# Retention on one Trainium2 core: gate projection split in halves, group deviation by a power on GpSimd

## The reference, cut to what matters

```
qkv = x @ w_qkv; q, k, v = split(qkv)          # x is the layer norm of the residual stream
q = xpos(q); k = xpos(k)                       # rotary tables, 16 heads of 32 columns
scores = einsum('bhtd,bhsd->bhts', q, k) * D ** (-0.5) * decay_mask
y = einsum('bhts,bhsd->bhtd', scores, v)
yn = (y - mean(y)) / sqrt(var(y) + EPS)        # over the 32 columns of one head
out = (silu(x @ w_g) * (yn * gn_weight + gn_bias)) @ w_proj
```

## Time and profile before

| | |
|---|---|
| median of 3 runs | 367.62 us (366.87 to 367.95) |
| the profiled execution | 367.68 us, span 365.8 us |
| PE busy | 355.6 us, 97% of the span |
| DVE, ACT, POOL busy | 145.2, 91.2, 35.7 us |
| retention's projections (first L1499) | from 293.12 us |
| value products end | 311.15 us |
| first gated transposes | from 314.26 us |
| output projection ends | 319.10 us |

### The profile page before, as it was taken

The page is one execution under the profiler, slowest core; times in us unless marked ns, Lnnn a source line. Parts: engine busy times, 40 slices in busy tenths (PEclk is TensorE's granted clock), DMA queues, the critical chain, the costliest instruction groups (busy, mean ns, idle before and its releaser), DMA issues.

```text
span 365.8 us, 5114 instructions
## 1 busy us (share of the span) xinstructions
PE 355.6 (97%) x2079; PEld 217.4 (59%) x2079; DVE 145.2 (40%) x319; ACT 91.2 (25%) x181; POOL 35.7 (10%) x72
## 2 busy tenths in 40 slices
PE   7898999999999999999999999999999999999997
PEld 6797677777778565756544443344356545554455
DVE  2128555777552126436103212311356344563131
ACT  1011344556442002311312221221113025130110
POOL 1005000000000010011000000000028310011210
PEclk9999999999999999999999999999999999999999
DMA  7999999900002500025489898899969920000000
GB/s 255 426 419 443 421 422 429 404 20 2 0 2 67 222 0 2 2 63 225 168 349 438 343 418 351 341 406 381 442 243 423 426 101 0 2 0 0 0 0 30
DMA packets 7799, 79.41 MB, mean 217 GB/s; under 512 B 992, under 2 KB 1760, under 8 KB 2912
## 3 DMA queue, kind: packets, MB, share of 16 engines
q1 hardware_dynamic: 7776, 79.09, 52.8%
HBM read 78.82 MB, written 0.26 MB: 216 GB/s over the span
## 4 chain that ended last, share of the span: by engine, by line
PE 88%; DVE 5%; DMA 3%; issue 1%; ACT 1%; SPq 1%; ACTq 0%
PE ps L1395 10%; PE ps L1568 9%; PE ps L1132 8%; PE ps L1155 7%; PE ps L1422 4%; PE ps L1224 4%; PE ps L1499 4%; PE ps L1144 4%; PE ps L1382 4%; PE ps L1441 3%; DMA ra<-in_wq 3%; PE ps L1355 3%; PE ps L1082 2%; PE ps L1337 2%; PE ps L1433 2%; PE ps L1275 2%
## 5 line engine op out<-in xcount | busy, mean ns | idle before, releaser
L1395 PE MATMUL ps<-rd,ra 128*64 128x384 f32 x224 | 38.9, 489 | 0.0
L1155 PEld LDWEIGHTS ps<-rd,ra 128*128 128x128 f32 x256 | 29.9, 192 | 4.4 <-issue 4.1
L1155 PE MATMUL ps<-rd,ra 128*128 128x128 f32 x256 | 31.3, 275 | 0.0
L1132 PE MATMUL ps<-rd 128*128 128x512 f32 x64 | 30.2, 594 | 0.0
L1395 PEld LDWEIGHTS ps<-rd,ra 128*64 128x64 f32 x224 | 15.5, 137 | 24.3 <-issue 24.3
L892 DVE SCALAR_TENSOR_TENSOR ra<-ra,ps 128x192 f32<-128x192 f32 x14 | 5.0, 354 | 61.3 <-ACT ra L567 61.3
L1568 PE MATMUL ps<-rd,xnT 128*128 128x512 f32 x64 | 28.0, 593 | 0.0
L476 ACT ACTIVATE ra<-ps,sv 128x1024 f32<-128x1024 f32 x16 | 17.8, 1114 | 35.1 <-DVE sv L718 35.1
L1033 PE MATMUL ps<-ones 128*128 128x256 bf16 x177 | 24.9, 286 | 1.0 <-POOL ones L397 1.0
L718 DVE TENSOR_REDUCE sv<-ps 128x1 f32<-128x1024 f32 x16 | 19.6, 1222 | 12.5 <-PE ps L1132 12.5
L1033 PEld LDWEIGHTS ps<-ones 128*128 128x128 bf16 x177 | 17.6, 102 | 7.0 <-issue 3.4
(11 more groups left out here) (260 smaller groups left out, 504.7 us busy)
## 6 DMA issues: line engine op xcount, KB each, us to landing
rd<-in_ring SPq DMA_DIRECT2D x7, 2560.0 KB, 8.7
rd<-in_ring SPq DMA_DIRECT2D x7, 2048.0 KB, 9.6
rd<-in_f1gu SPq DMA_DIRECT2D x8, 1024.0 KB, 13.1
rb<-in_wb SPq DMA_DIRECT2D x1, 5120.0 KB, 34.6
ra<-in_e SPq DMA_DIRECT2D x2, 2560.0 KB, 16.6
rb<-in_b SPq DMA_DIRECT2D x1, 5120.0 KB, 21.2
ra<-in_wr SPq DMA_DIRECT2D x4, 1152.0 KB, 16.3
rd<-in_ring SPq DMA_DIRECT2D x2, 2304.0 KB, 14.6
```

The source lines that it names most:

```text
L1132: ins = pe.matmul(ps[:, 2 * (u % 2) + half, :], rows, kvT[:, u % 2, half * 512:half * 512 + 512], start=True, stop=True)
L1155: ins = pe.matmul(ps[:, 6, 0:P], probT_x[u % 2][:, j, :], kvr[:, u % 2, j, :], start=(j == 0), stop=(j == J - 1))
L1395: ins = pe.matmul(ps[CAP * e:CAP * e + CAP, 2 + p % 2, 0:2 * I0].rearrange("p (g n) -> p g n", g=2), moe_xq[q % 2][:, c, CAP * e4:CAP * e4 ...
```

## The change

The gate projection (t = 3) is split into halves of 256 columns. The first, for heads 0 to 7, stays where the whole one was; the second is issued behind the value products, ahead of the residual. The 18 fillers behind the residual become 3. The tanh is split too: the second half stands behind the squares in ScalarE's list. VectorE forms ret_ag, ret_aw and ret_ab for the first half only, in the old place.

Sqrt, its dummy and the reciprocal go. GpSimd takes the power of the 16 variances with exponent -0.5 and writes g_rstd; it does so between its memset of ret_v and the next layer norm's `rstd_of(5)`. The squares wait for VectorE's multiplication of the first half only. VectorE multiplies the second half of y by gn_weight alone, behind the scalar step of the variance, so while GpSimd takes the power. After the division it adds gn_bias to the second half, waits for the second tanh, forms the second half of ret_ag and multiplies by it last; then PE may transpose that half.

```diff
--- before.py
+++ after.py
@@ -196,8 +196,8 @@
         w_retv = w_ret[:, :, 2, :].rearrange("p c (h d) -> p c h d", h=16)
         w_retv_mean = ra[:, 3104:3168].rearrange("p (c h) -> p c h", c=C)
         w_sum = ra[:, 3168:3680].rearrange("p (c h d) -> p c h d", c=2, h=16)
-        ret_aw = ra[:, 9792:10304]
-        ret_ab = ra[:, 10304:10816]
+        ret_aw = ra[:, 9792:10048]
+        ret_ab = ra[:, 10304:10560]
         ret_oT = ra[:, 9280:9792].rearrange("p (c t) -> p c t", c=C)
         decay = ra[:, 11264:11776].rearrange("p (c n) -> p c n", c=C)
 
@@ -290,9 +290,9 @@
         g_ps, u_ps, th_done, h_done, hT_ps, hT_sb, dn_done = map(
             sem, ("g_ps", "u_ps", "th_done", "h_done", "hT_ps", "hT_sb", "dn_done"))
         placed_w_done, xq_ps, xq_sb, y_sb, moe_done = map(sem, ("placed_w_done", "xq_ps", "xq_sb", "y_sb", "moe_done"))
-        t_ps, rot_done, ret_v_sb, ret_th_done, ret_T_ps, ret_T_sb, qbd_done, rs_ps, ret_pT_sb, y_ps, yw_var_done, sq_sqrt_done = map(
+        t_ps, rot_done, ret_v_sb, ret_th_done, ret_T_ps, ret_T_sb, qbd_done, rs_ps, ret_pT_sb, y_ps, yw_var_done, sq_pow_done = map(
             sem, ("t_ps", "rot_done", "ret_v_sb", "ret_th_done", "ret_T_ps", "ret_T_sb", "qbd_done", "rs_ps", "ret_pT_sb", "y_ps",
-                  "yw_var_done", "sq_sqrt_done"))
+                  "yw_var_done", "sq_pow_done"))
         ret_o_done, ret_oT_ps, ret_oT_sb, proj_ps = map(
             sem, ("ret_o_done", "ret_oT_ps", "ret_oT_sb", "proj_ps"))
         fr_ps, frmx, frexp, fcoef, fcT_ps, fcT_sb, fck_ps, mix_done = map(
@@ -443,6 +443,8 @@
             ins.then_inc(v_zero, 1)
             rstd_of(4)
             pool.memset(ret_v, 0.0).then_inc(v_zero, 1)
+            pool.wait_ge(yw_var_done, 2)
+            pool.tensor_tensor(g_rstd[:, :], g_var, neghalf.broadcast_to([P, 16]), ALU.pow).then_inc(sq_pow_done, 1)
             rstd_of(5)
 
             pool.wait_ge(fh, 1)
@@ -596,8 +598,12 @@
             for hh in range(4):
                 act.activation(ret_qbd[:, :, hh, :], ps[:, 4, :].rearrange("p (c t) -> p c t", c=C), ACT.Copy,
                                scale=m32[:, hh:hh + 1]).then_inc(qbd_done, 1)
-            act.wait_ge(t_ps, 3)
-            act.activation(ret_th, ps[:, 3, :], ACT.Tanh, scale=half_rstd).then_inc(ret_th_done, 1)
+            def gate_tanh(half):
+                act.wait_ge(t_ps, 3 + 2 * half)
+                cols = slice(256 * half, 256 * half + 256)
+                act.activation(ret_th[:, cols], ps[:, 3, cols], ACT.Tanh, scale=half_rstd).then_inc(ret_th_done, 1)
+
+            gate_tanh(0)
             act.wait_ge(ret_T_ps, 2)
             act.activation(ret_kT.rearrange("p c t -> p (c t)"), ps[:, 5, :], ACT.Copy).then_inc(ret_T_sb, 1)
             act.wait_ge(t_ps, 4)
@@ -606,15 +612,12 @@
                 for b in range(B):
                     src = ps[S * b:S * b + S, 2, :].rearrange("p (g two d) -> p two g d", g=8, two=2)
                     act.activation(ret_v[S * e:S * e + S, b, :, e, :], src[:, e], ACT.Copy).then_inc(ret_v_sb, 1)
-            act.wait_ge(consts_ready, 2)
-            act.activation(mix[:, 20:21], ones[:, 0:1], ACT.Sqrt)
+            act.wait_ge(yw_var_done, 1)
             for half in range(2):
                 act.wait_ge(y_ps, half + 1)
-                act.wait_ge(yw_var_done, half + 1)
                 act.activation(ret_sq[:, 8 * half:8 * half + 8, :].rearrange("p h d -> p (h d)"), ps[:, 4 + half, 0:256],
-                               ACT.Square).then_inc(sq_sqrt_done, 1)
-            act.wait_ge(yw_var_done, 3)
-            act.activation(g_rstd[:, :], g_var, ACT.Sqrt).then_inc(sq_sqrt_done, 1)
+                               ACT.Square).then_inc(sq_pow_done, 1)
+            gate_tanh(1)
             act.wait_ge(ret_oT_ps, 1)
             act.activation(ret_oT[:, 0:2, :].rearrange("p c t -> p (c t)"), ps[:, 0, 0:256], ACT.Copy).then_inc(ret_T_sb, 1)
 
@@ -932,10 +935,12 @@
                                                    ALU.mult, ALU.mult)
                 link(ins)
                 dve.tensor_tensor(rot[:, t], rot[:, t], rot_tmp[:, t], ALU.add).then_inc(rot_done, 1)
+            col_a, col_b = slice(0, 256), slice(256, 512)
+            head_a, head_b = slice(0, 8), slice(8, 16)
             dve.wait_ge(ret_th_done, 1)
-            link(dve.scalar_tensor_tensor(ret_ag, ret_th, 1.0, ps[:, 3, :], ALU.add, ALU.mult))
-            link(dve.scalar_tensor_tensor(ret_aw, ret_ag, half_rstd, gnwb[:, 0, :], ALU.mult, ALU.mult))
-            link(dve.scalar_tensor_tensor(ret_ab, ret_ag, half_rstd, gnwb[:, 1, :], ALU.mult, ALU.mult))
+            link(dve.scalar_tensor_tensor(ret_ag[:, col_a], ret_th[:, col_a], 1.0, ps[:, 3, col_a], ALU.add, ALU.mult))
+            link(dve.scalar_tensor_tensor(ret_aw, ret_ag[:, col_a], half_rstd, gnwb[:, 0, col_a], ALU.mult, ALU.mult))
+            link(dve.scalar_tensor_tensor(ret_ab, ret_ag[:, col_a], half_rstd, gnwb[:, 1, col_a], ALU.mult, ALU.mult))
             dve.wait_ge(ld_decay, 16)
             for m in range(2):
                 dve.wait_ge(rs_ps, m + 1)
@@ -944,21 +949,29 @@
                                   ALU.mult).then_inc(ret_pT_sb, 1)
 
             yf = ret_y.rearrange("p h d -> p (h d)")
-            halves = [(slice(256 * half, 256 * half + 256), slice(8 * half, 8 * half + 8)) for half in range(2)]
-            for half, (cols, _) in enumerate(halves):
-                dve.wait_ge(y_ps, half + 1)
-                dve.tensor_tensor(yf[:, cols], ps[:, 4 + half, 0:256], ret_aw[:, cols], ALU.mult).then_inc(yw_var_done, 1)
-            for half, (_, heads) in enumerate(halves):
-                dve.wait_ge(sq_sqrt_done, half + 1)
+
+            dve.wait_ge(y_ps, 1)
+            dve.tensor_tensor(yf[:, col_a], ps[:, 4, 0:256], ret_aw, ALU.mult).then_inc(yw_var_done, 1)
+            for half, heads in enumerate((head_a, head_b)):
+                dve.wait_ge(sq_pow_done, half + 1)
                 ins = dve.tensor_reduce(g_var[:, heads], ret_sq[:, heads, :], AX.X, ALU.add)
             link(ins)
             dve.tensor_scalar(g_var, g_var, 1.0 / 32, EPS, ALU.mult, ALU.add).then_inc(yw_var_done, 1)
-            dve.wait_ge(sq_sqrt_done, 3)
-            link(dve.reciprocal(g_rstd[:, :], g_rstd[:, :]))
-            for cols, heads in halves:
+            link(dve.tensor_tensor(yf[:, col_b], ps[:, 5, 0:256], gnwb[:, 0, col_b], ALU.mult))
+
+            def divide_heads(heads):
                 link(dve.tensor_tensor(ret_y[:, heads, :], ret_y[:, heads, :],
                                        g_rstd[:, heads].unsqueeze(2).broadcast_to([P, 8, 32]), ALU.mult))
-                dve.tensor_tensor(yf[:, cols], yf[:, cols], ret_ab[:, cols], ALU.add).then_inc(ret_o_done, 1)
+
+            dve.wait_ge(sq_pow_done, 3)
+            divide_heads(head_a)
+            dve.tensor_tensor(yf[:, col_a], yf[:, col_a], ret_ab, ALU.add).then_inc(ret_o_done, 1)
+            divide_heads(head_b)
+            link(dve.tensor_tensor(yf[:, col_b], yf[:, col_b], gnwb[:, 1, col_b], ALU.add))
+            dve.wait_ge(ret_th_done, 2)
+            link(dve.scalar_tensor_tensor(ret_ag[:, col_b], ret_th[:, col_b], 1.0, ps[:, 3, col_b], ALU.add, ALU.mult))
+            dve.scalar_tensor_tensor(yf[:, col_b], ret_ag[:, col_b], half_rstd, yf[:, col_b], ALU.mult,
+                                     ALU.mult).then_inc(ret_o_done, 1)
             dve.wait_ge(ret_oT_ps, 2)
             dve.tensor_copy(ret_oT[:, 2:4, :].rearrange("p c t -> p (c t)"), ps[:, 6, 0:256]).then_inc(ret_oT_sb, 1)
 
@@ -1499,6 +1512,12 @@
                     ins = pe.matmul(ps[:, t, :], xnT[:, c, :], w_ret[:, c, t, :], start=(c == 0), stop=(c == C - 1))
                 ins.then_inc(t_ps, 1)
 
+            def gate_projection(half):
+                cols = slice(256 * half, 256 * half + 256)
+                for c in range(C):
+                    ins = pe.matmul(ps[:, 3, cols], xnT[:, c, :], w_ret[:, c, 3, cols], start=(c == 0), stop=(c == C - 1))
+                ins.then_inc(t_ps, 1)
+
             def rotated_transposes(t):
                 pe.wait_ge(rot_done, t + 1)
                 for c in range(C):
@@ -1508,7 +1527,7 @@
             projection(0)
             projection(1)
             rotated_transposes(0)
-            projection(3)
+            gate_projection(0)
             rotated_transposes(1)
             pe.wait_ge(v_zero, 3)
             projection(2)
@@ -1533,8 +1552,9 @@
                                     ret_v[:, b, g].rearrange("p two d -> p (two d)"), start=True, stop=True)
                 if g % 4 == 3:
                     ins.then_inc(y_ps, 1)
+            gate_projection(1)
             residual(1, 4, True)
-            keep_clock(18, 2)
+            keep_clock(3, 2)
             src = ret_y.rearrange("p h d -> p (h d)").rearrange("p (c q) -> p c q", c=C)
 
             def gated_transposes(half):
```

## The result

| | before | after |
|---|---|---|
| median | 367.11 us (366.30 to 368.37, 20 runs) | 369.17 us (367.30 to 371.02, 20 runs) |
| ratio | | 1.005, 95% interval 1.0035 to 1.0065 |
| profiled execution, its span | 367.68, 365.8 us | 370.10, 368.2 us |
| GpSimd busy | 35.7 us | 38.6 us |
| mean granted clock | 1.000 | 0.995 |

The change makes the kernel slower by half a per cent, 1.8 us by the ratio. The last row of the table is the yardstick for all that follows: from the start of the first projection to the end of the output projection. It holds all that the change touches and leaves out what differs from run to run ahead of it (the projections began 0.21 us later in this execution). It is 293.12 to 319.10 before, and 293.33 to 321.51 after.

The account below looks back on a forecast made before the run. PE's own work bounds the kernel up to the value products, then the normalisation's latency until the first gated transposes. The terms sum to -1.95 + 1.15 = -0.80 us, from 367.68 to 366.9 us, range 365.9 to 370.0.

Parts of the forecast that it names:

- no change: Whole kernel: time within about 1.1 us of before, p from 0.85 to 3.05; chance 0.42 with rival 3.
- Step 1: Projections: half a gate projection leaves PE's stretch, so the value projection ends 1.31 us earlier, after a wait for the rotation.
- Step 2: From y to the variance: VectorE's scalar step ends at 311.23, 1.51 us earlier, 0.20 more than step 1 gave.
- Step 3: Normalisation: GpSimd's power replaces Sqrt and reciprocal, 0.57 us, by a link of 0.13 + p.
- p: GpSimd's time for the power of 128x16, put at 1.15 us, with 38 ns a column.
- -1.95 + p: Change in when the first gated half is ready, in us: 312.26 + p against 314.21 before.
- Rival 2: GpSimd's power is paid by the column, so PE waits: slower, 369.3 us at 200 ns a column; chance 0.24.
- Step 4: Second half gated last: PE waits 0.65 us for the first half, the added projection costs nothing, 0.3 us left for the second.
- Step 5: ScalarE's two table loads of 1283 ns, for Sqrt and the next Exp, may go; neither on the path, nothing won.
- rival 3: ScalarE's squares don't fit the tanh's table: two loads come in, both hidden, time stays the forecast's; chance 0.02.

Follow-up runs that it names:

- The widths: Kernel before, with GpSimd products and powers of 1 to 32 columns added in its idle time; powers took 0.57 to 5.42 us, one execution 366.83 us.
- Sqrt kept and trimmed: Changed kernel with Sqrt and reciprocal instead of the power, without the 3 fillers and the dummy Tanh; median 365.87 us, ratio 0.9963 to the kernel before.
- the Sqrt kernel: Changed kernel with Sqrt and reciprocal instead of the power, a dummy Tanh behind the Sqrt, 3 fillers kept; median 365.64 us, ratio 0.9949 to the kernel before.

## Why the prediction was wrong, point by point

The forecast was -0.80 and "no change"; measured is +1.8 by the ratio, inside the range but on the side to which it gave 0.24. Two of its terms failed: the power was sized at 1.15 us and took 2.93, and the idle time that this leaves PE was given no price, where it cost about 0.9 us in the mean of the runs. The first alone makes +0.98, a loss that the prediction still counted as no change; only with the second is the kernel clearly slower.

- **Step 1 held.** Forecast: the value projection ends 1.31 earlier. Measured: 303.24 + 3.44 = 306.68, less the 0.21 of the later start 306.47, against the forecast's 306.45. The wait for the rotation and the refill to 0.66 are both there.
- **Step 2 held, with 0.19 to spare.** Forecast: scalar step done at 311.23. Measured: 311.25 - 0.21 = 311.04. I set the first reduction 0.14 behind its square, the distance of before; but before, VectorE was still at its second multiplication then (311.18 to 311.61). Now the reduction starts 0.02 behind the square, and the two take 0.76 together (L957) where I counted 0.82.
- **Step 3's link held.** 0.07 us from VectorE to GpSimd, and about 0.1 back to the division at 314.36. That is 0.17 where 0.13 was forecast. With the measured p the formula -1.95 + p gives +0.98; the first gated half moved by +0.83, 0.15 less: step 2's 0.19 less the 0.04 here.
- **The term that failed first is p.** I put the power's growth between 3 and 381 ns a column and took the middle by ratio as 38 ns (it is 34, which would make p 1.08). Measured are 156 ns, and p is 2.93 instead of 1.15: 1.78 us, which turns -0.80 into +0.98. I called 1.15 nearer by far to the measured row, but that row has one column. It could not say how its 381 ns over the product divide. The widths say: about 155 recur with each column and some 225 are paid once.
- **Rival 2 had the mechanism**, and its break-even of 92 ns a column was passed: 156 ns. The Trainium skill's charge for a dependent chain in each element (GPSIMD Engine Reference, "Performance pitfalls for Q7 kernels") pointed the right way, but not by its size: its 4 cycles are, as an estimate at that page's 1.2 GHz, 3.3 ns. What that page gives for a two-input operation, by estimate 2.2 ns, is near the product's 1.7 here and far from the power's 156. No run shows what the power does inside.
- **The second term that failed is the price of PE's idle time.** The prediction asked about the clock only for 5.8 us of it, though it named a lower clock from 312 to 317 as a sign of being wrong. Step 4 said that the fillers replaced "were worth nothing either". That was wrong for a PE that waits: with p = 2.93 its idle time is 2.13 us, and the clock fell in 11 of 20 executions, in none of 12 with the gap filled, and cost 1.37 us in the profiled one. The prediction had the price of a fall, up to 3.7 us, but not the place where it begins to matter. Whether the wait of 0.65 us in its own forecast would have brought a fall, no run tests.
- **Step 4's cover for the second half held.** It was ready at 317.00 and PE asked at 318.28, with its clock down; at full clock, with Sqrt kept and trimmed, it was ready at 315.22 and PE asked at 315.55, 0.33 against the 0.3 forecast. The added half projection cost nothing.
- **Step 5 and rival 3.** Behind 0.72 us the changed kernel has no table load at all, so Square does fit the tanh's table, and rival 3 falls. The loads cost nothing before, and neither of the two in the Sqrt kernel is in its chain of waits, though the tanh behind the second is done only 0.04 ahead of the copy.

## What to carry to other kernels

When an operation is to be used at a new width, one measured row at width one bounds nothing useful: put a ladder of widths into idle time of that engine first, at no cost that was seen here. Judge the parts of a change one by one: this one holds a split that wins 1.5 us and a power that loses 2.4 to 2.5, and the first without the second beats the kernel before by half a per cent and the changed one by a whole one. When a chain of waits grows longer beside a waiting PE, its fillers have to grow with it, or the clock can add its own price; and a slow operation that can't be made shorter may still be cut, so that only its first part is on the path.

## What the hardware showed that I had not expected

- GpSimd's power with exponent -0.5: 0.57, 0.70, 1.01, 1.64, 2.90, 5.42 us for 1, 2, 4, 8, 16, 32 columns of 128 partitions, a straight line of 156 ns a column, beside 0.24 us for the product of 32 columns.
- TensorE idle for 2.13 us in the changed kernel: the mean clock was 0.995 in 11 of 20 executions, in none of 12 with that gap filled, and in none of 39 of the four other variants that kept TensorE at work. With 2.06 us of idle time in the kernel before it was so in 4 of 12, against 2 of 26 with the fillers there, which is too few to be sure. In the one fall that a trace shows the clock was at the lower level from about 315.6 to 319.0 us, beginning just after TensorE had taken up work again. Executions with the fall were 1.4 to 1.6 us longer.
